# A two-block network on one core: gates inside the value and residual products, one chain for both gates, bf16 three-part biases, and a new order of steps

## The chip, the cores and the metric

The kernel runs on one core of a Trainium2 chip. Its time is the device time of one launch in microseconds (us). The median of three runs of the kernel before is 563.08 us (561.6 to 563.08). PE is TensorE, DVE is VectorE, ACT is ScalarE, POOL is GpSimd and SP is SyncE. Each engine runs its own instructions in the order in which they are written, and engines wait for each other on semaphores.

## The reference

Input x is 16 sequences of 256 tokens of 128 features, 4096 tokens in all. Two blocks follow each other; each is `x = x + s * silu(ffn)` with s and ffn computed from the layer norm of x.

```python
# block 0
xn = layernorm(x)
q, k, v = xn @ W_qkv.T                       # per sequence, linear attention
q, k = relu(q) + eps, relu(k) + eps
s = (q @ (k.T @ v)) / (q @ sum(k) + eps) @ W_out.T + b_out
gates = softmax(xn @ gate_w)                 # 8 experts, 2 largest
tok_w = sum of the 2 largest; sel = which experts
ffn = tok_w * sum over the selected e of (gelu(xn @ w1[e] + b1[e]) @ w2[e] + b2[e])   # 64 hidden each
x = x + s * silu(ffn)
# block 1
xn = layernorm(x)
K, V, Q = xn @ theta_K.T, xn @ theta_V.T, xn @ theta_Q.T
for each token of a sequence:                # TTT layer, a recurrence over 256 tokens
    g = 2/128 * (W @ k + b - v);  W -= LR * outer(g, k);  b -= LR * g;  s = W @ q + b
P = softmax(xn @ Wg), the 2 largest, normalised to sum 1
ffn = sum over the selected e of P[e] * (gelu(xn @ W1[e] + b1[e]) @ W2[e] + b2[e])    # 512 hidden each
x = x + s * silu(ffn)
```

## The kernel before

**Tiles and groups.** A tile is 128 tokens; four tiles (two sequences) are a group, and there are 8 groups. Everything is fp32 unless said otherwise, and a TensorE product in fp32 shows as two matmul instructions.

**The first pass** works through the groups in periods. Its order of steps is written out by hand in `PERIOD` (L318) and `CLOSE` (L328), and every engine walks the same lists in `first_pass` (L340) and does its part of each step in its own `work`. A step has a stage letter; in period p stage A works on group p, B on p-1, C on p-2 and D on p-3 (`LAG`, L316). A is block 0's norm (`ln0`), transposes (`xt0`), gate logits (`lg0`), attention (`k`, `v`, `q`, `kv`, `att`), the choice of experts (`sel0`, `tok0`) and its transpose (`selT`). B is block 0's experts (`hid0 0` to `hid0 3`, `y0`), the sum into x (`mix0`), block 1's norm (`ln1`), transposes (`xt1`) and gate logits (`lg1`). C is the first half of the TTT layer, solved as a triangular system per tile: key and query products (`kT`, `qT`), their Gram matrices (`gram_n`, `gram_q`, `gram_x`), the right-hand side (`resid`), and the inverse built up in levels of doubling block size (`half1`/`join1` to `half3`/`join3`), and beside it gate 1 (`sel1`, `pw1`), each token's rank in its experts (`rank`), and the sending of token rows to the experts' regions in DRAM (`copies`, `send 0` to `send 3`: indirect DMAs from POOL's queue). D is levels 4 to 6 (`half4` to `join6`, with the transposes `turn`), the two solves (`u1`, `cross`, `u2`) and the output `out`. PE does the products, ACT copies most results out of PSUM, DVE does norms, gates, masks and the joins, POOL adds biases and masks on SBUF and sends.

**Both gates** run the same chain of small DVE operations of 32 elements per partition, one after the other in a period: `shifted` (L1146), `two_largest` (L1156), `softmax` (L1173). Their logits are products of their own with 8 columns (L678, L745).

**Biases of block 0's experts.** `hid0` adds 0 or minus HUGE to hidden units of experts not chosen by a bf16 product with `selT_b` (L726); `y0` adds the output bias by an fp32 product of `selT` and `b2_l0` (L734).

**The unit stage.** When all rows are sent, expert by expert, units of 256 rows are loaded from DRAM into a ring of four by SP (L419 to L426), transposed on PE (`turn`, L854), multiplied (`hid`, L861: 4 products of 256 columns), put through gelu on ACT (`gelus`, L1036), multiplied again (`out`, L874: 8 products of 128 columns), biased and weighted on DVE (`results_of`, L1357) and scattered to DRAM by POOL (`send_results`, L583). h1T, the gelu results of one unit, is a single buffer: gelu j of the next unit waits until `out` has counted `h1_free` for k = j. On PE the order is hid(u+1), turn(u+2), out(u), hid(u+2), and hid waits for gelus of the unit before it, since their PSUM banks are reused. The first eight units stand in `CLOSE`, interleaved with the last D steps; the rest are loops. 36 units run in all.

**The end** reads the results back, adds the two choices of each token, takes silu, multiplies by the TTT output and adds to x.

## Time and profile before

| What | us |
|---|---|
| median of 3 runs | 563.08 |
| profiled execution, whole | 563.21 |
| its span, first to last instruction | 561.5 |
| one full period of the first pass (217.80 to 256.07) | 38.27 |
| the loops of the unit stage (424.18 to 529.60) | 105.42 |
| mean granted clock of TensorE, share of full speed | 0.932 |

The span is the time between the first and the last instruction of the core. The profile gives for each engine its busy time, and for TensorE the clock it was granted, as a share of 2.4 GHz (1.00 is 2.4 GHz, 0.50 is 1.2 GHz). Matmuls are pipelined: the distance between the starts of two steps is what the first of them costs; the busy time of a step also holds its tail.

### The profile page before, as it was taken

What the parts mean: (1) busy time and instruction counts of PE and PEld (TensorE: products, weight loads), DVE (VectorE), ACT (ScalarE), POOL (GpSimd) and SP (SyncE); (2) the same over time, 40 slices, a digit from 0 to 9 for tenths busy, and PEclk for the clock granted to TensorE, in tenths of its full rate; (3) what the DMA queues carried; (4) which work ended last, traced back from release to release, by engine and by line L of the source; (5) the groups of instructions that cost most, each with busy time, mean ns of one, the idle gap of its engine ahead of it and who ended that gap; (6) DMA issues with size and microseconds to landing.
All of it is one profiled execution on the core that took longest, in us unless ns stands there. A gap on an engine that the chain in (4) does not pass through costs nothing. (4 is left out here: it accounts for less than half of the span.)

```text
span 561.5 us, 10856 instructions
## 1 busy us (share of the span) xinstructions
PE 486.9 (87%) x3342; PEld 421.1 (75%) x3342; DVE 340.4 (61%) x1326; ACT 219.0 (39%) x494; POOL 211.7 (38%) x288
## 2 busy tenths in 40 slices
PE   5559588899999999999999996878999999999724
PEld 2437477689798797897897985777989899898711
DVE  6344679789888898898886766221233334434427
ACT  2233333334434424434345221113365565554502
POOL 9200131441633624516327246300454545544510
PEclk9989889899999999999999987577999999999957
DMA  7995000000000000000000001320222222222267
GB/s 201 327 165 64 0 2 11 19 11 11 21 11 11 21 21 10 20 11 20 11 11 19 20 16 39 79 51 1 56 54 69 67 71 75 68 68 62 63 223 244
DMA packets 36575, 32.58 MB, mean 58 GB/s; under 512 B 5248, under 2 KB 29358, under 8 KB 36527
## 3 DMA queue, kind: packets, MB, share of 16 engines
q1 hardware_dynamic: 31808, 22.96, 17.2%
q0 software_dynamic: 4352, 8.99, 4.9%
q8 instruction: 25, 0.41, 0.3%
q14 instruction: 24, 0.19, 0.1%
q10 hardware_dynamic: 366, 0.04, 0.1%
HBM read 16.63 MB, written 15.34 MB: 57 GB/s over the span
## 5 line engine op out<-in xcount | busy, mean ns | idle before, releaser
L588 POOL DMA_INDIRECT results<-nat,y_to x72 | 70.4, 978 | 87.4 <-DVE nat L1377 73.0
L571 POOL DMA_INDIRECT routed<-send,slot x64 | 63.0, 984 | 69.8 <-DVE slot L1298 46.1
L868 PE MATMUL psA<-xuT,w_all 128*128 128x256 f32 x288 | 71.3, 393 | 2.8 <-ACT h1T L1043 2.4
L1043 ACT ACTIVATE h1T<-psA,b1T 128x256 f32<-128x256 f32 x144 | 63.8, 474 | 5.0 <-PE psC L880 2.1
L1349 DVE TENSOR_SCALAR xu<-ring 128x256 f32 (+1 forms) x38 | 11.3, 296 | 84.0 <-DMA ring<-routed 60.6
L868 PEld LDWEIGHTS psA<-xuT,w_all 128*128 128x128 f32 x288 | 52.7, 198 | 11.0 <-issue 2.0
L880 PE MATMUL psB<-w_all,h1T 128*128 128x128 f32 x288 | 56.5, 278 | 1.8 <-DVE nat L1362 1.5
L880 PE MATMUL psC<-w_all,h1T 128*128 128x128 f32 x288 | 55.7, 275 | 0.0
L880 PEld LDWEIGHTS psB<-w_all,h1T 128*128 128x128 f32 x288 | 43.6, 192 | 3.2 <-issue 3.1
L880 PEld LDWEIGHTS psC<-w_all,h1T 128*128 128x128 f32 x288 | 43.7, 192 | 0.0
L1034 ACT ACTIVATE xuT<-psB 128x256 f32<-128x256 f32 x37 | 14.2, 383 | 61.9 <-PE psB L858 31.0
L580 POOL TENSOR_TENSOR s<-s,bias_rows 128x512 f32<-128x512 f32 x8 | 10.1, 1261 | 67.9 <-ACT s L1029 67.9
L733 PE MATMUL psB<-w_l,hg0T 128*128 128x128 f32 x256 | 34.3, 277 | 0.8 <-ACT hg0T L978 0.8
L725 PE MATMUL psB<-xnT,w_l 128*128 128x512 f32 x64 | 34.7, 626 | 0.0
L576 POOL TENSOR_TENSOR s<-s,bias_rows 128x512 f32<-128x512 f32 x8 | 10.1, 1265 | 62.8 <-ACT s L972 62.8
L733 PEld LDWEIGHTS psB<-w_l,hg0T 128*128 128x128 f32 x256 | 31.2, 192 | 1.5 <-ACT hg0T L978 1.5
L813 PE MATMUL psC<-xinvT,pn 128*128 128x64 f32 x192 | 28.1, 295 | 3.2 <-issue 2.0
L799 PEld LDWEIGHTS psD<-xinv,nT 128*128 128x128 f32 x192 | 25.6, 203 | 6.0 <-issue 3.7
L813 PEld LDWEIGHTS psC<-xinvT,pn 128*128 128x128 f32 x192 | 26.7, 215 | 3.9 <-issue 3.8
L799 PE MATMUL psC<-xinv,nT 128*128 128x64 f32 x192 | 28.0, 293 | 1.7 <-DVE xinv L1321 1.5
L799 PE MATMUL psD<-xinv,nT 128*128 128x64 f32 x192 | 26.7, 285 | 2.0 <-DVE xinv L1321 1.2
L799 PEld LDWEIGHTS psC<-xinv,nT 128*128 128x128 f32 x192 | 25.9, 209 | 3.3 <-DVE xinv L1321 2.2
(248 smaller groups left out, 1075.8 us busy)
## 6 DMA issues: line engine op xcount, KB each, us to landing
ring<-routed SPq DMA_DIRECT2D x38, 130.0 KB
w_all<-results SPq DMA_DIRECT2D x16, 256.0 KB, 5.1
routed<-ring SPq DMA_DIRECT2D x24, 130.0 KB, 9.1
w_all<-in_L_ffn_W_dram SPq DMA_DIRECT2D x1, 2048.0 KB, 14.9
out_dram<-x_all SPq DMA_DIRECT2D x8, 256.0 KB, 2.3
results<-nat,y_to POOLq DMA_INDIRECT x72
routed<-fill SPq DMA_DIRECT2D x8, 130.0 KB, 3.8
routed<-send,slot POOLq DMA_INDIRECT x64
```

The costliest lines, as they stand in the source:

```text
L571: pool.indirect_dma_start(routed[:, :], bass.IndirectOffsetOnAxis(ap=slot[par][:, c, t:t + 1], axis=0), send[par][c][:, t, :], None).then_ ...
L576: pool.tensor_tensor(s0[par][:, :, :], s0[par][:, :, :], four(bias_rows[:, 0, :]), ALU.add).then_inc(S["s0_ready"], 1)
L588: pool.indirect_dma_start(results[:, :], bass.IndirectOffsetOnAxis(ap=y_to[:, par, a:a + 1], axis=0), yw[:, par, a, :], None).then_inc(S[f ...
L725: mm(psB[j % 2][:, :], w, xT0[:, :], start=True, stop=False)
L733: mm(o, hg0T[:, j, t * P:(t + 1) * P], w2_l0[:, j, :], start=(j == 0), stop=False)
L799: last = mm(packed(bank, lv)[:, t], nT[par][:, t, :], blocks(xinv[par], lv, 0)[:, t], start=True, stop=True)
L813: last = mm(packed((psC, psD)[c][1], lv)[:, t], pn[c][:, t, :], blocks(xinvT[par], lv, 1)[:, t], start=True, stop=True)
L868: last = mm(psH[j // 2][:, (j % 2) * UNIT:(j % 2 + 1) * UNIT], w1_all[:, e, j * P:(j + 1) * P], xuT[:, :], start=True, stop=True)
L880: last = mm(psY[a][:, 0:D], h1T[:, k, a * P:(a + 1) * P], w2_all[:, f * JF + k, :], start=(k == 0), stop=(k == JF - 1))
L1034: f(xuT[:, :], psX[:, 0:UNIT], ACT.Copy).then_inc(S["xuT_ready"], 1)
L1043: f(h1T[:, j, :], psH[j // 2][:, (j % 2) * UNIT:(j % 2 + 1) * UNIT], ACT.Gelu, bias=b1T[:, n:n + 1]).then_inc(S["gelu_ready"], 1)
L1349: v.tensor_scalar(xu[:, :, :], ring[:, bass.ds(u % RING, 1), :, 0:D].rearrange("p r a d -> p (r a) d"), 1.0, None, ALU.mult).then_inc(S["x ...
```

## The change

- **Gates in other products.** gate_w stands behind the value product's weights and Wg behind the residual product's: `v` and `resid` have 136 columns instead of 128, and `lg0`, `lg1` have no products of their own. `resid` moves from stage C to a stage X, right behind `xt1`. Their results lie in pairs of tiles over two banks.
- **Both gates as one.** A stage G does gate 0 of group p and gate 1 of group p-2 in one chain of operations of 64 elements per partition (`floor`, `sel`, `tok`). Stage R does ranks, slots, copies and sends.
- **Biases of block 0 in bf16.** The output bias is split into three bf16 parts that add up to it. One bf16 transpose of the choices, each three times beside a constant one, serves both `hid0` (four bf16 products of 128 columns for one of 512) and `y0` (one bf16 product per tile for one in fp32). DVE makes the parts in the opening, from twelve small loads.
- **TTT one period later**: C has lag 3 and D lag 4. `xt1` has lag 2: it stands in the period after its norm. The close has C for groups 6 and 7 and D for groups 5, 6 and 7.
- **Norm of block 0.** Moments and inverse roots of all tiles behind the first group are made in period 0; `ln0` is four scaled copies.
- **Masks, subtraction and bias sums** of `gram_q`, `resid`, `att` and `out` go from ACT and POOL to one DVE operation each, straight out of PSUM where they were there; `gram_x` is two ACT operations. `selT` is one ACT copy.
- **Level 6** works on 64x64 blocks (`half6`, `join6`), and `join6` is an ACT copy.
- **rank** is 5 bf16 products in place of 18.
- **Unit stage.** `out` does half a = 0 over all k, then a = 1, both in one bank, and DVE adds the bias in one operation.
- **Start and hand-over.** Biases come by broadcast loads instead of products; PE starts on the identity alone; SP writes the filling rows before it waits for the sent rows.
- **New order of steps** in `PERIOD` and `CLOSE`, and an own list for period 0.

```diff
+LAG = {"S": 0, "A": 0, "G": 0, "B": 1, "R": 2, "C": 3, "D": 4, "X": 2}
+OPEN0 = (
+    "A xt0", "A v", "A ln0", "S products", "S b2", "A lg0", "G floor", "G sel", "S stats1", "S stats2", "A k",
+    "S stats3", "S stats4", "A q", "A selT", "A kv", "S stats5", "G tok", "A att", "S stats6", "S stats7",
+    "S roots", "A bias0",)
+PERIOD = (
+    "D half4", "C kT", "X xt1", "C qT", "C one", "A ln0", "R landed", "D join4", "C gram_n", "A xt0",
+    "X resid", "D half5", "X lg1", "C gram_q", "A lg0", "A v", "C gram_x", "D join5", "R copies", "B hid0 0",
+    "G floor", "C half1", "G sel", "D turn", "B hid0 1", "A q", "D half6", "C join1", "B hid0 2", "D join6",
+    "B hid0 3", "D u1", "C half2", "R rank", "A k", "R slots", "D cross", "A selT", "C join2", "B y0",
+    "C half3", "D u2", "G tok", "R send 0", "A kv", "B mix0", "R send 1", "C join3", "A att", "B ln1",
+    "R send 2", "R send 3", "A bias0", "D out",)
+CLOSE = (
+    "5 half4", "6 qT", "6 kT", "7 xt1", "7 landed", "5 join4", "6 gram_q", "6 gram_n", "5 half5", "7 resid",
...
+    "7 gram_q", "7 gram_x", "6 join5", "7 half1", "6 turn", "7 join1", "6 half6", "6 join6", "7 half2", "6 u1",
+    "U first", "7 join2", "7 send 1", "7 one", "U hid 0", "6 cross", "7 send 2", "7 half3", "6 u2", "U gelu 0",
+    "7 send 3", "7 join3", "6 out", "U sent", "7 half4", "U hid 1", "7 join4", "U out 0", "7 half5", "U hid 2",
...
@@ SP @@
+            sp.wait_ge(fill_in, 16 * E)
             wait_on(sp, "rows_landed", groups)
-            for e in range(E):
-                sp.dma_start(routed[bass.ds(free[e], UNIT), :].rearrange("(a p) d -> p a d", p=P),
-                             fill[:, e % 2, :, :]).then_inc(fill_in, 16)
-            sp.wait_ge(fill_in, 16 * E)
@@ PE work @@
                     for t in range(TILES):
-                        last = mm(psA[1][:, t * E:(t + 1) * E], xT0[:, t * P:(t + 1) * P], gate0[:, :],
-                                  start=True, stop=True)
...
+                        last = mm(pairs(psA)[:, t // 2, t % 2, 0:D + E], xT0[:, col(t)], wv_gate0[:, :],
                                   start=True, stop=True)
                     last.then_inc(S["v0_ps"], 1)
...
-                    mm(psB[j % 2][:, :], expert_of[:, j, :], selT_b[par][:, :], start=False,
-                       stop=True).then_inc(S["hid0_ps"], 1)
+                    for t in range(TILES):
+                        last = mm(psB[:, j % 2, col(t)], expert_of[:, t, j, :], selT[par][:, :], start=False,
+                                  stop=(t == TILES - 1))
+                    last.then_inc(S["hid0_ps"], 1)
...
-                        last = mm(o, selT[par][:, t * P:(t + 1) * P], b2_l0[:, :], start=False, stop=True)
+                        last = mm(o, selT[par][:, :], b2_x[:, t, :], start=False, stop=True)
...
+                elif step == f"half{LEVELS - 1}":
+                    for t in range(TILES):
+                        last = mm(psD[HALF:P, 0, t * HALF:(t + 1) * HALF], nT[par][0:HALF, t, HALF:P],
+                                  xinv[par][0:HALF, t, 0:HALF], start=True, stop=True)
...
@@ PE out(u, f, e) of the unit stage @@
                 wait_on(pe, "yb_ready", u)
-                for k in range(JF):
-                    wait_on(pe, "gelu_ready", u * JF + k + 1)
-                    for a in range(HALVES):
-                        last = mm(psY[a][:, 0:D], h1T[:, k, a * P:(a + 1) * P],
+                for a in range(HALVES):
+                    for k in range(JF):
+                        if a == 0:
+                            wait_on(pe, "gelu_ready", u * JF + k + 1)
+                        last = mm(psB[:, 1, col(a)], h1T[:, k, a * P:(a + 1) * P],
                                   w2_all[:, f * JF + k, :], start=(k == 0), stop=(k == JF - 1))
-                    last.then_inc(S["h1_free"], 1)
+                        if a:
+                            last.then_inc(S["h1_free"], 1)
@@ DVE work @@
+                elif step == "ln0":
+                    if g == 0:
+                        moments(stats0, mv0, 0, TILES, 0)
+                        inverse_roots(rstd0, mv0, 0, TILES)
+                    else:
+                        wait_on(dve, "xt0_ps", g)
+                    normalise(xn, g * TILES, mv0, rstd0, g * TILES, "xn0_ready")
...
+                elif step == "sel":
+                    ready("d_ready")
+                    ts = gate_tiles(g)
...
+                elif step == "tok":
...
+                    v.tensor_tensor(gates_of(tok_w[par]), m, z, ALU.mult).then_inc(S["tok_ready"], 1)
+                    if g >= GATES_LAG:
+                        c = slice(TILES, GT)
+                        ready("tok_ready")
+                        link(v.tensor_scalar(norm[:, :], tok_w[par][:, c], NORM_EPS, None, ALU.add))
...
+                        v.tensor_tensor(send[(g - GATES_LAG) % 2][:, :, :, COL_W], top[:, :, c],
+                                        twice(norm[:, :]), ALU.mult).then_inc(S["weights_ready"], 1)
...
+                elif step == "resid":
+                    ready("res_ps")
+                    v.tensor_tensor(by_pair(res[g % XBUFS][:, :, :]), pairs(psB)[:, :, :, 0:D],
+                                    by_pair(four(cb0[:, :])), ALU.subtract).then_inc(S["res_ready"], 1)
```

## Rows read from the trace of the kernel before

**Rows 1.** The page: busy us (share of the span) and instructions.

```profile
PE 486.9 (87%) x3342; PEld 421.1 (75%) x3342; DVE 340.4 (61%) x1326; ACT 219.0 (39%) x494; POOL 211.7 (38%) x288
```

**Rows 2.** Stages: length, busy time per engine (instructions), clock, DMA share, GB/s.

```profile
217.80:256.07 38.27, 37.39 (x298) 32.77 (x298) 33.14 (x129) 16.07 (x37) 15.60 (x17) 1.00 0.05 15
...
330.98:379.16 48.18, 36.62 (x210) 33.91 (x210) 20.05 (x72) 8.31 (x19) 20.03 (x22) 0.71 0.23 53
...
379.16:424.18 45.02, 41.89 (x279) 38.30 (x279) 11.32 (x53) 19.91 (x49) 14.21 (x15) 0.93 0.15 40
...
424.18:529.60 105.42, 102.79 (x704) 92.66 (x702) 41.95 (x192) 60.09 (x138) 52.83 (x55) 1.00 0.25 68
```

**Rows 3.** PE in order, one full period: start, busy, step, wait before.

```profile
226.85 0.95 PE L678 MATMUL psA<-gate,xnT 128*128 128x8 f32 x8
...
227.66 1.08 PE L799 MATMUL psD<-xinv,nT 128*128 128x64 f32 x8
...
233.56 0.46 PE L821 MATMUL psD<-ident,xinvT 64*128 64x64 f32 x4
...
233.95 1.11 PE L799 MATMUL psC<-xinv,nT 128*128 128x64 f32 x8
...
237.62 0.39 PE L734 MATMUL psB<-b_l,selT 128*128 128x128 f32 x2
...
237.85 1.06 PE L733 MATMUL psB<-w_l,hg0T 128*128 128x128 f32 x8
...
241.20 0.20 PE L755 MATMUL psB<-sel_b,before 128*128 128x8 bf16 x2
...
241.56 1.14 PE L683 MATMUL psA<-wkT,xnT 128*128 128x128 f32 x8
...
250.09 0.60 PE L706 MATMUL psA<-ident,sel 128*8 128x128 f32 x4
```

**Rows 4.** DVE in order, the same period.

```profile
244.71 0.69 DVE L1248 TENSOR_TENSOR mix<-s,gg 128x512 f32<-128x512 f32 x1
...
248.77 0.85 DVE L1121 BATCH_NORM_STATS2 stats<-x_all 128x6 f32<-128x128 f32 x4
...
252.58 1.11 DVE L1142 TENSOR_SCALAR send<-x_all,mv,rstd 128x128 f32<-128x128 f32 x4
```

**Rows 5.** ACT in order, the same period.

```profile
241.40 1.14 ACT L984 ACTIVATE gg<-psB,tok_w 128x128 f32<-128x128 f32 x4 [5.03 <-PE psB L734]
```

**Rows 6.** PE in order: the waits before xt0 in two periods.

```profile
71.33 0.95 PE L673 MATMUL psA<-ident,xn 128*128 128x128 f32 x4 [2.09 <-DVE xn L1142]
...
224.39 0.65 PE L673 MATMUL psA<-ident,xn 128*128 128x128 f32 x4 [0.88 <-DVE xn L1142]
```

**Rows 7.** Stretches around waits of PE, columns as in rows 2.

```profile
318.00:322.00 4.00, 3.26 (x22) 3.10 (x22) 3.36 (x9) 0.50 (x2) 2.09 (x2) 0.84 0.10 33
...
406.00:412.00 6.00, 4.92 (x37) 4.51 (x36) 1.44 (x7) 2.81 (x8) 2.24 (x3) 1.00 0.13 33
...
68.00:76.00 8.00, 5.91 (x31) 4.70 (x29) 4.94 (x18) 2.23 (x4) 1.26 (x2) 0.79 0.01 3
```

**Rows 8.** PE in order: the first transposes of the pass.

```profile
18.58 1.09 PE L673 MATMUL psA<-ident,xn 128*128 128x128 f32 x4 [3.51 <-POOL mask_lv L520]
```

**Rows 9.** PE in order: the first and the last hid of the loops.

```profile
420.45 1.89 PE L868 MATMUL psA<-xuT,w_all 128*128 128x256 f32 x8
...
524.57 1.89 PE L868 MATMUL psA<-xuT,w_all 128*128 128x256 f32 x8
```

**Rows 10.** PE in order: out of one unit and the next hid.

```profile
460.30 0.39 PE L880 MATMUL psB<-w_all,h1T 128*128 128x128 f32 x2
...
460.52 0.39 PE L880 MATMUL psC<-w_all,h1T 128*128 128x128 f32 x2
...
462.08 1.89 PE L868 MATMUL psA<-xuT,w_all 128*128 128x256 f32 x8
```

**Rows 11.** ACT in order: the four gelus beside them.

```profile
460.95 1.81 ACT L1043 ACTIVATE h1T<-psA,b1T 128x256 f32<-128x256 f32 x4
```

More of the change, by code:

```diff
@@ L356, in first_pass @@
                 else:
-                    g = groups - 2 if stage == "D" else groups - 1
-                    work(step, g, g % 2)
+                    work(step, int(g))
         MAX_UNITS = (CHOICES * tokens) // UNIT + MIN_UNITS * E
@@ new lines, in work @@
+                    ready("selb_ready")
+                    if g + GATES_LAG < groups:
+                        wait_on(pe, "q0_ready", g + GATES_LAG + 1)
+                    else:
+                        wait_on(pe, "s0_raw", groups)
+                        if g + GATES_LAG > groups:
+                            wait_on(pe, "rank_read", g)
+                    mm(rank_ps, before[:, :], sel_b[:, :], start=True, stop=False)
+                    for s in range(TILES):
+                        rest = TILES - s
+                        last = mm(rank_ps[:, (s + 1) * E:].rearrange("p (t e) -> p t e", e=E), ones_b[:, :],
+                                  sel_b[:, s * E:(s + 1) * E].unsqueeze(1).broadcast_to([P, rest, E]),
+                                  start=False, stop=(s == TILES - 1))
@@ new lines, in moments, with inverse_roots @@
+            def moments(stats, mv, first, n, x_first):
+                for t in range(n):
+                    last = v.bn_stats(stats[:, first + t, :], x_all[:, x_first + t:x_first + t + 1, :])
+                link(last)
+                for t in range(n):
+                    last = v.bn_aggr(mv[:, first + t, :], stats[:, first + t, :])
+                link(last)
+            def inverse_roots(rstd, mv, first, n):
+                ts = slice(first, first + n)
+                r, a, ve, sd = rstd[:, ts], nt_a[:, 0:n], var_e[:, 0:n], seed[:, 0:n]
+                link(v.tensor_scalar(ve, mv[:, ts, 1], LN_EPS, None, ALU.add))
+                link(v.tensor_scalar(sd, ve.bitcast(I32), 1, None, ALU.logical_shift_right))
+                link(v.tensor_scalar(r.bitcast(I32), sd, -1.0, float(RSQRT_SEED), ALU.mult, ALU.add))
@@ L1187, in ready, with work @@
+            def work(step, g):
+                par = g % 2
+                group = slice(g * TILES, (g + 1) * TILES)
                 def ready(name, per=1, k=1):
                     wait_on(dve, name, g * per + k)
-                def link_in(stage):
-                    def link(ins):
-                        ins.then_inc(order[stage], 1)
-                        links[stage] += 1
-                        dve.wait_ge(order[stage], g * CHAIN[stage] + links[stage])
-                    return link
@@ L1298, in work @@
+                    ready("rank_read")
+                    link(v.tensor_tensor(pick[:, :, c], choice[:, :, c], twice(place[:, :, :]), ALU.mult))
+                    link(v.tensor_reduce(slot_f[:, :, :], pick[:, :, c], AX.X, ALU.add))
                     v.tensor_copy(slot[par][:, :, :], slot_f[:, :, :]).then_inc(S["slots_ready"], 1)
-                    assert links["C"] == CHAIN_C, links
-                    if isinstance(g, int) and g == groups - 1:
+                    if g == groups - 1:
@@ L1360, in results_of @@
                 wait_on(dve, "yw_ready", u)
[L1361 to L1363 removed]
+                v.tensor_tensor(yb[:, :, :], tiles(psB[:, 1, :], HALVES),
+                                b2_all[:, f:f + 1, :].broadcast_to([P, HALVES, D]),
+                                ALU.add).then_inc(S["yb_ready"], 1)
                 wait_on(dve, "y_landed", u - 1)
```

882 lines of the change are left out of this document (437 added, 445 removed), and 21 rows, old and new, of tables (CLOSE, PERIOD).

## The prediction

> **What bounds the kernel now.** I read the page first: TensorE (PE) is busy 87% of the span, VectorE (DVE) 61% [rows 1]. That is an average over stages, so I cut the span into stages next [rows 2]. A full period of the first pass (all four stages A to D in it) lasts 38.27 us, with PE busy 37.39 and DVE 33.14: PE bounds it, and DVE has little to spare. There are five such periods in a row, equal within 0.02 us. The close (330.98 to about 420) is different: from 330.98 to 379.16 the granted clock is 0.71, so PE is neither full nor fast. The unit stage has PE busy 102.79 of 105.42 at clock 1.00: pure PE. Then I read one period in order of time, where the distance from one start to the next is what a step costs PE (the busy column holds the pipeline's tail and overstates it).
>
> The profiled execution took 563.21 us for a span of 561.5, so 1.7 lies around it; the median of the runs shown, 563.08, is the same number for this purpose. I sum against 563.2.
>
> **PE work in a period.** Four logit products of 8 columns cost 227.66 - 226.85 = 0.81, as much as four of 128 columns would: eight passes of 0.1. Both gates' sets go (2 x 0.81), and the value and residual products grow from 128 to 136 columns, 6% on about 0.9 each, +0.1: together -1.5. y0's bias product costs 237.85 - 237.62 = 0.23 per tile in fp32; in bf16 it is one pass instead of two and one column a cycle: priced by hid0's bf16 products (512 columns at 0.22) it is 0.06. Four tiles: -0.7. The four selection transposes (L706, 0.60 long) become one [rows 3]: -0.3. rank goes from 18 instructions in 0.36 to 5: -0.25. hid0's bf16 product of 512 columns becomes four of 128 with four weight loads; rank's 18 products with a load each take 20 ns apiece, so loads don't bound it: 0, at worst +0.1 per step, +0.4 a period. half6 and join6 work on 64x64 blocks: each between 0 and 0.45 less than their 0.85; I take 0.2 each, -0.4. Sum: -3.2 of some 37.1, so 33.9 of PE work in a full period (bounds 33.4 to 34.6).
>
> The Trainium skill ("TensorEngine Tiling (Array Packing)", Key Properties) says that a change of tiling mode drains TensorE, which speaks against the 64x64 form of half6 and join6. The one 64x64 step here, the turn, takes 233.95 - 233.56 = 0.39 for four passes, 0.1 each although only 64 columns wide, which fits a small drain [rows 3]. By that rule alone the two steps gain nothing, and a period would be 0.4 longer, 1.6 over four.
>
> **DVE work in a period.** Removed: the first norm's moments and roots (the second norm's, 252.58 - 248.77 = 3.8, are the same instructions [rows 4]), one of two gate chains (about 3.6 of 9.5: the links stay, with 64 elements instead of 32), join6's copy 0.45. Added: masks, subtraction and two bias sums that POOL or ACT did, four operations of 512 elements at 0.69 (as L1248 [rows 4]): +2.7. DVE falls from 33 to about 29 busy; ACT loses some 3. POOL loses five operations of 1.27. None of these is on the path by its total; the order is.
>
> **Where the period waits then.** The new order puts xt1 third in the next period, and it waits for the second norm, the last long work of DVE. I walk from the start Y of y0. PE: y0 3.8, half3 0.9, u2 0.5, kv 0.9, join3 0.9, att 0.95, out 2.4, half4 0.85, kT 0.95: xt1 could start at Y+12.1. ACT: y0 lands at Y+4.0, scaled copy 1.14 [rows 5] to 5.2, then half3, u2 and kv stand before the tanh of mix0, which ends at 7.3. DVE: k, slots (1.05), cross, join2 end at Y+2.3, the merged softmax and weights (14 links, 3.2) at 5.5, mix0 three operations of 0.69 with the second waiting for the tanh: 8.75; join3 1.1, att 0.4, norm 4.9 (moments from 248.77 to the last of the four outputs, 253.69 [rows 4]): Y+15.15. So xt1 waits 3.0. If DVE never waited it would be 13.4 and the wait 1.25. I take 2.2.
>
> Idle time has a second price. After 2.09 us without work the granted clock went to half rate for about 3.5 us (a mean of 0.79 in the 8 us around it), but not after the 0.88 of every full period, nor after 1.08 (4.92 busy of 6.00) [rows 6, 7]. 2.2 lies at the first of these: half the periods, at 1.7 each. Period: 33.9 + 2.2 + 0.9 = 37.0; bounds 35.2 (1.25 and no slow clock) and 38.7 (3.05 and always). Four such periods instead of five 38.27: per period -1.27, over the four -5.1.
>
> **The thin periods.** TTT one period later leaves periods 2 and 3 thinner. Before, the second norm of group 0 is done at 61.65 and that of group 2 at 138.9 (one period before 177.2, two before 215.4, three before 253.69): 77.3. With no C and D in period 2 my walk (xt1, ln0, xt0, resid, v at half rate, hid0, q, k, y0, tail) gives 25.3; period 3 has C but not D, 33.5. Together 58.8, so -18.5. Period 8 has no A: 33.1 against 34.5, -1.4. The thinned work comes back in the close.
>
> **Opening.** PE's first transposes waited 3.51 for POOL's masks until 18.58 [rows 8]; now they wait for the identity alone and start near 13.4, 5.2 earlier. But DVE then has the split of the bias (17 operations, 4.0), and moments and roots of 28 tiles (seven of about 1.4, whose statistics are 0.85 [rows 4], and 2.5 of roots: 12.3, 7.5 more than one group's 4.8). These fall partly into DVE's waits. hid0 of group 0 no longer fills the gap before period 1. By walk, group 0's second norm is done at 63.8 instead of 61.65: +2 (bounds -3, all hidden, and +6, nothing hidden). The twelve bias loads end before DVE asks for them, unless the large weight loads hold them up.
>
> **Close.** Before: from the norm of group 7 (326.5) to the first hid of the loops (420.45 [rows 9]) 94.0, with 59.3 of full-rate PE work; 34.7 are lost, over half of it at half rate. After: C and D of groups 6 and 7, D of 5: 75.6 of work. Two chains alternate, PE has something to do in most gaps: my walk has PE at the first turn after 34, with 3.4 of gaps, and the rows are sent in time (slots at +16.4, eight sends of 1.27, then 3 to 6 to land; the fillings no longer follow them). I add 4 for half rate, 7 for unit waits and chain ends: lost 14.4, close 90. -4 (bounds -11, lost 7, and +16, lost 34.7).
>
> **Unit stage.** out used to do both halves for each k; now half a=0 runs over all k, then a=1, and only a=1 frees h1T. Before: out starts at 460.30, its fourth pass for k=0 ends at 460.52 + 0.39 = 460.91, gelu starts at 460.95, 0.65 after out's start [rows 10, 11]. Now k=0 is free after passes 9 and 10: 4 x 0.223 + 0.39 = 1.28, gelu at 1.32 to 1.39, two gelus 0.42 + 0.47, done at 2.28, and PE answers 0.14 later: the next hid starts 2.42 after out's start, not 462.08 - 460.30 = 1.78. So +0.63 per unit, at every unit, because PE had no idle time and gelu sits in the loop. 27 steps from 420.45 to 524.57 [rows 9]: +17 (bounds: +12 if some of the 3.3 of odd waits there are hidden in it, +17).
>
> **Sum.** +2 - 18.5 - 5.1 - 1.4 - 4 + 17 = -10.0: 553.2.
>
> **Rivals.** (1) Slower: the clock. The wait before xt1 takes its full 3.05 and the half rate lasts 6.8 us each time, as it did from 320.6 to 327.4 in period 8 (the fall is in [rows 7]): 33.9 + 3.05 + 3.4 = 40.35 per period, +13.4 over four and +3.4 in periods 3 and 8: 570. It turns the sign from a period of 39.5 on. For it: the fall in period 8 came after two waits of about 0.5 only. Against: full periods hold 1.00 through 0.88. (2) The unit wait does not come, since gelu is not held as I think: -17, 536. For it: nothing but my reading of one semaphore; against, gelu's start 0.04 after the fourth pass [rows 10, 11]. (3) No wait before xt1, PE bounds the period at 34.0: -3.0 times four and -2.8 twice, 535.6. For it: my durations on DVE are strung together; against, even DVE without waits is late. (4) The close loses its 34.7 as before (DVE in order behind a late unit load, half rate again): +20, 573.5. For it: it has more steps of 64 columns, which ran at 0.71.
>
> Chances: forecast 0.42 (its own range 543 to 563), (1) 0.17, (2) 0.12, (3) 0.14, (4) 0.15. About 0.3% is what a measurement of this kernel tells from no change, here 561.4 to 564.8. Faster: 0.35 of the forecast's and the 0.26 of (2) and (3), 0.61; the same 0.09, the forecast's upper end and the mild ends of (1); slower 0.30. The range that leaves 2 in 10 out: 535 to 573.
>
> **What would show it.** Opening: L673's successor near 13.4. A full period 35 to 39 long with PE waiting at xt1 on DVE's norm, and a granted clock under 1.00 there. The logit products gone, y0 near 3.8. Unit stage: starts of hid 4.37 apart instead of 3.73, PE idle before each on ACT's h1T. Close: granted clock above 0.8. I am wrong if hid stays at 3.73, or if xt1 starts right behind kT.

## The result and the profile after

The kernel before takes 559.5 us (median of 20 runs, 553.3 to 564.7), the changed kernel 562.7 us (20 runs, 560.0 to 567.3). The ratio is 1.008, 95% interval 1.0056 to 1.0103: the change makes the kernel 0.8% slower. The forecast was 553.2, so the sign was wrong, though the time lies inside the range. Its -10.0 was counted from 563.2, the level of the first three runs; from 559.5 it would have been 549.5.

The profiled execution of the changed kernel took 561.8 us for a span of 560.0. That of the kernel before, with 563.2, is above most of its own 20 runs; so I compare a second pair of profiles too, taken on one chip (runs before_same_chip and after_same_chip below). First the page of the changed kernel, part 1, then the granted clock in 40 slices of the span (9 stands for 90% of full speed or more):

```profile
PE 466.1 (83%) x3176; PEld 396.9 (71%) x3176; DVE 306.9 (55%) x1097; ACT 188.7 (34%) x464; POOL 168.5 (30%) x251
...
PEclk9767697978989999979989958799999999999968
```

Against [rows 1] TensorE (PE) has 20.8 us less to do, VectorE (DVE) 33.5, and nothing came of it: the busy share fell, the time did not. The stages say where it went. This is the view of stretches of the changed kernel, columns as in [rows 2]; the cuts are at the starts of xt1 for groups 0 to 7 (65.81 to 314.61), then inside the close, at the first hid of the loops (409.11) and at the last (524.07).

```profile
0.00:65.81 65.81, 30.39 (x153) 23.13 (x153) 43.47 (x197) 15.14 (x35) 20.66 (x83) 0.79 0.74 172
65.81:91.66 25.85, 19.00 (x118) 14.77 (x119) 17.75 (x73) 8.52 (x20) 6.79 (x9) 0.83 0.04 13
91.66:124.65 32.99, 29.92 (x201) 24.32 (x201) 23.61 (x83) 11.44 (x27) 10.91 (x14) 0.86 0.06 20
124.65:164.36 39.71, 36.66 (x276) 31.32 (x277) 26.23 (x87) 13.29 (x33) 9.85 (x14) 0.93 0.05 14
164.36:203.03 38.67, 35.63 (x276) 30.29 (x276) 26.31 (x88) 13.30 (x33) 9.91 (x13) 0.96 0.05 15
203.03:240.33 37.30, 34.25 (x277) 29.43 (x277) 26.25 (x88) 13.30 (x33) 9.98 (x13) 0.98 0.05 16
240.33:280.22 39.89, 36.84 (x276) 31.50 (x277) 26.47 (x88) 13.30 (x33) 9.91 (x13) 0.93 0.05 14
280.22:314.61 34.39, 32.15 (x239) 26.58 (x239) 21.94 (x77) 10.96 (x26) 10.04 (x12) 0.96 0.05 17
314.61:359.52 44.91, 42.23 (x283) 39.69 (x284) 24.39 (x77) 10.06 (x26) 10.73 (x14) 0.76 0.17 47
359.52:409.11 49.59, 45.52 (x322) 41.04 (x322) 15.00 (x50) 18.03 (x48) 11.60 (x12) 0.98 0.13 36
409.11:524.07 114.96, 107.97 (x703) 95.92 (x703) 38.87 (x163) 52.65 (x136) 51.99 (x54) 1.00 0.22 63
```

Two things are to be seen. The four full periods (124.65 to 280.22) execute the same instructions, 276 or 277 on PE, and last 37.30, 38.67, 39.71 and 39.89: they follow the clock column, 0.98, 0.96, 0.93, 0.93. Before, they were equal at 1.00. And the unit stage has PE waiting, 107.97 busy of 114.96 at clock 1.00, where it was all but full [rows 2].

The stages of both pairs, in us (before, then after):

| stretch | forecast | first pair | same-chip pair |
|---|---|---|---|
| opening, to xt1 of group 0 | +2 | 61.6, 65.8: +4.2 | 64.0, 67.9: +3.9 |
| the two thin periods | -18.5 | 77.3, 58.8: -18.4 | 79.4, 59.5: -19.9 |
| four full periods | -5.1 | 153.1, 155.6: +2.5 | 153.2, 155.8: +2.6 |
| xt1 of group 6 to the loops' first hid | -5.4 | 128.4, 128.9: +0.5 | 124.5, 128.9: +4.4 |
| 27 unit steps | +17 | 104.1, 115.0: +10.8 | 102.0, 115.0: +13.0 |
| tail | 0 | 36.9, 36.0: -0.9 | 36.5, 35.8: -0.7 |
| sum | -10 | -1.4 | +3.3 |

The last row is the difference of the spans; the rows above it are rounded one by one. The second pair agrees with the medians (+3.2). The thin periods gave what they were to give. The units took back the most, 10.8 to 13.0, then the opening with 4 and the full periods with 2.5. How much the close took depends on the profile of the kernel before: its own close was 3.9 us shorter in the second one.

Who ends the waits of PE shows in the view of waits of the changed kernel, first 124.65 to 314.61, then the unit stage (us in total, times, longest):

```profile
PE psB L712 <- DVE send L1141: 13.5, 5, 3.0
PE psC L802 <- ACT pn L1007: 0.3, 1, 0.3
```

```profile
PE psA L857 <- ACT h1T L1032: 7.3, 28, 0.3
```

The first is the wait before xt1 for the second norm, 3.05 for each of groups 3 to 6 (the fifth, 1.3, is that of group 2 at the edge). Before, no full period had it. The rows of these four waits (start, busy, step, wait before) show one more thing:

```profile
164.36 1.12 PE L712 MATMUL psB<-ident,send 128*128 128x128 f32 x4 [3.05 <-DVE send L1141]
203.03 0.66 PE L712 MATMUL psB<-ident,send 128*128 128x128 f32 x4 [3.04 <-DVE send L1141]
240.33 1.12 PE L712 MATMUL psB<-ident,send 128*128 128x128 f32 x4 [3.04 <-DVE send L1141]
280.22 1.12 PE L712 MATMUL psB<-ident,send 128*128 128x128 f32 x4 [3.05 <-DVE send L1141]
```

The same four transposes are busy 1.12 us behind three of the waits and 0.66 behind the one that ends at 203.03: there the clock stayed full, and no half rate is seen until 238.9, inside the next wait. That is the period of 37.30. So one trace already holds the same wait with and without half rate behind it. (The first full period, behind the wait of 1.3, is at half rate until 129.7; there the clock had fallen at 119.6, behind a wait of 1.76 before half4.)

The second row of the waits is the one before hid for the first gelus, once a unit. Outside these two, the view of waits shows 0.3 us in these stretches of PE.

### The profile page after: what moved, and what is told of

It reads as the page before. It is cut to its first block, busy times and chain, and to the rows that moved or that the text cites. A ratio compares the mean times of both kernels' runs of the same rounds, so it can differ in the third digit from the quotient of the medians.

```text
span 560.0 us, 10211 instructions
## 1 busy us (share of the span) xinstructions
PE 466.1 (83%) x3176; PEld 396.9 (71%) x3176; DVE 306.9 (55%) x1097; ACT 188.7 (34%) x464; POOL 168.5 (30%) x251
## 4 chain that ended last, share of the span: by engine, by line
PE 66%; DVE 16%; issue 5%; ACT 5%; DMA 3%; ACTq 2%; POOL 1%; SPq 0%; DVEq 0%; POOLq 0%
PE psA L857 13%; PE psB L870 7%; PE psB L694 6%; PE psB L706 5%; PE psC L788 4%; PE psC L802 4%; ACT h1T L1032 3%; PE psD L802 2%; DVE stats L1122 2%; PE psC L747 2%; PE psA L647 1%; PE psC L751 1%; PE psB L847 1%; DVE send L1141 1%; PE psD L788 1%
## 5 line engine op out<-in xcount | busy, mean ns | idle before, releaser
L551 POOL DMA_INDIRECT routed<-send,slot x64 | 65.9, 1030 | 191.9 <-DVE send L1250 141.5
L870 PE MATMUL psB<-w_all,h1T 128*128 128x128 f32 x576 | 70.5, 275 | 0.6 <-ACT h1T L1032 0.6
L870 PEld LDWEIGHTS psB<-w_all,h1T 128*128 128x128 f32 x576 | 67.1, 192 | 0.9 <-ACT h1T L1032 0.8
L857 PEld LDWEIGHTS psA<-xuT,w_all 128*128 128x128 f32 x288 | 52.6, 193 | 20.8 <-ACT h1T L1032 12.6
L1032 ACT ACTIVATE h1T<-psA,b1T 128x256 f32<-128x256 f32 x144 | 56.4, 474 | 26.4 <-PE psB L870 26.4
L962 ACT ACTIVATE hg0T<-psB,b1T 128x512 f32<-128x512 f32 x32 | 22.0, 687 | 33.3 <-PE psB L696 33.3
L712 PE MATMUL psB<-ident,send 128*128 128x128 f32 x32 | 8.0, 398 | 26.7 <-DVE send L1141 26.7
L712 PEld LDWEIGHTS psB<-ident,send 128*128 128x128 f32 x32 | 5.1, 198 | 33.4 <-DVE send L1141 33.4
L1386 DVE TENSOR_TENSOR nat<-psB,b_all 128x256 f32<-128x256 f32 x36 | 15.3, 424 | 23.6 <-PE psB L870 23.6
L696 PEld LDWEIGHTS psB<-selT,expert_of 128*128 128x128 bf16 x128 | 10.0, 99 | 18.9 <-issue 18.9
L1341 DVE STREAM_TRANSPOSE xinv<-xinvT 128x512 f32<-128x512 f32 x32 | 22.8, 712 | 1.1
```

The source lines that it names most:

```text
L551: pool.indirect_dma_start(routed[:, :], bass.IndirectOffsetOnAxis(ap=slot[par][:, c, t:t + 1], axis=0), send[par][:, c, t, :], None).then_ ...
L857: last = mm(psA[:, j // 2, (j % 2) * UNIT:(j % 2 + 1) * UNIT], w1_all[:, e, j * P:(j + 1) * P], xuT[:, :], start=True, stop=True)
L870: last = mm(psB[:, 1, col(a)], h1T[:, k, a * P:(a + 1) * P], w2_all[:, f * JF + k, :], start=(k == 0), stop=(k == JF - 1))
L962: f(hg0T[:, j, :], psB[:, j % 2, :], ACT.Gelu, bias=b1T[:, HT + j:HT + j + 1]).then_inc(S["hg0_ready"], 1)
L1032: f(h1T[:, j, :], psA[:, j // 2, (j % 2) * UNIT:(j % 2 + 1) * UNIT], ACT.Gelu, bias=b1T[:, n:n + 1]).then_inc(S["gelu_ready"], 1)
L1341: v.transpose(xinv[par][:, :, :], xinvT[par][:, :, :]).then_inc(S[f"xinv{lv}_ready"], 1)
```

## The experiments

Each edit is shown against the kernel named; the step lists are shared by all engines.

**The unit stage.** out_k_outer undoes one part of the change, before_a_outer does that part alone.

```
 # out_k_outer, in out() of the changed kernel
-for a in range(HALVES):
-    for k in range(JF):
-        if a == 0: wait_on(pe, "gelu_ready", u * JF + k + 1)
-        last = mm(psB[:, 1, col(a)], h1T[:, k, ...], ...)
-        if a: last.then_inc(S["h1_free"], 1)
+for k in range(JF):
+    wait_on(pe, "gelu_ready", u * JF + k + 1)
+    for a in range(HALVES):
+        last = mm((psB[:, 1, 0:P], psC[:, 0, 0:P])[a], h1T[:, k, ...], ...)
+    last.then_inc(S["h1_free"], 1)
```

> The changed kernel with one part undone: in the unit stage the second product (out) runs k outermost again, both halves of the unit for each k, each half in a PSUM bank of its own, and h1T is given back after every k (and so two bias additions of 128 columns on VectorE where there was one of 256). Theory A, the unit order is a cost of its own: TensorE waits 0.4 to 0.5 us before each hid on ACT's first gelus only because h1T comes free after the whole first half. Then the step of a unit goes from 4.26 to 3.73 us, 27 steps and the seven outs in the close with it: 10.8 less in the stage, up to 3 more in the close, so 548 to 552. Rival B: the units are longer because of something else that the change did (the extra work of the close behind them, unit loads that come late, the one bias addition): then the step stays above 4.1 and the time is 560 to 563.

> The kernel before with this part alone done: out runs half a=0 over all k and then half a=1, and h1T is given back only from the second half; the two PSUM banks and the two bias additions stay. Theory A: the step of a unit goes from 3.73 to about 4.26 us and the kernel is 11 to 17 us slower than before (27 steps of 0.41 to 0.63), 570 to 576. Rival B (the order costs nothing by itself, TensorE's own work in the step bounds it): 559 to 562.

Measured: out_k_outer 555.1 us, ratio to the kernel before 0.9785 (0.974 to 0.983); before_a_outer 578.8, ratio 1.022 (1.0175 to 1.0263). The kernel before took 568.3 us beside these two, on another chip. The changed kernel was not measured there, so neither the times nor the ratios can be set against its own exactly; the stage itself can. By the loops' stretch (out_k_outer first, then before_a_outer, columns as in [rows 2]):

```profile
414.10:517.89 103.79, 102.72 (x704) 92.41 (x703) 40.56 (x188) 58.87 (x136) 51.47 (x54) 1.00 0.25 69
```

```profile
424.00:539.82 115.82, 108.48 (x706) 96.01 (x705) 39.95 (x191) 53.61 (x138) 53.27 (x55) 1.00 0.23 62
```

The one edit takes 27 steps from 115.0 to 103.8, the other puts the old kernel from 104.1 to 115.1 (the stretch shown begins 0.7 ahead of the first hid). Both directions are seen, and the step is 4.26 with and 3.8 without, whatever stands around it. The rival is out. (late_xt1_k_outer below does the same edit beside its partner on one chip: 550.9 to 536.2.) How the 4.26 comes about, by PE in order in the changed kernel (start, busy, step, wait), and ACT beside it:

```profile
460.20 1.99 PE L857 MATMUL psA<-xuT,w_all 128*128 128x256 f32 x8 [0.26 <-ACT h1T L1032]
462.03 0.38 PE L847 MATMUL psB<-ident,xu 128*128 128x128 f32 x2
462.25 1.95 PE L870 MATMUL psB<-w_all,h1T 128*128 128x128 f32 x16
464.46 0.48 PE L857 MATMUL psA<-xuT,w_all 128*128 128x256 f32 x1 [0.26 <-ACT h1T L1032]
```

```profile
463.57 1.20 ACT L1032 ACTIVATE h1T<-psA,b1T 128x256 f32<-128x256 f32 x3 [0.73 <-PE psB L870]
```

out starts at 462.25, the first gelu 1.32 later, the next hid 2.21 later; before, 0.65 and 1.78 [rows 10, 11]. PE, ACT and the one buffer h1T form a ring with little slack: the first gelu starts 0.67 later behind out, and the next hid 0.43 later.

**The wait before xt1 and the clock behind it.** tanh_first exchanges "A kv" and "B mix0" in PERIOD. fill_pe sets useless products before the wait:

```
 elif step == "xt1":
+    for _ in range((6, 5, 1, 3, 3, 3, 3, 0)[g]):
+        mm(psB[:, 1, :], wqT, xT0[:, :], start=True, stop=True)
     ready("xn1_ready")
```

> The changed kernel with two neighbours in the period's order exchanged: mix0 now stands before kv, so ACT does the tanh of the gate before the copy of kv. Theory A: the tanh is late behind kv, the middle of mix0 on VectorE waits for it, the second norm ends with it and TensorE waits for the norm before xt1. Then the wait of 3.05 us before xt1 falls by about one copy, 0.6 to 0.8, and the period by that or more: 0.8 times five periods, 4, so 557 to 559.5; more, to 553, if the half rate behind the wait goes too. Rival B: VectorE's own work bounds the chain (k, slots, cross, tok, join3, att before and in it) and the tanh is not late by that much: wait 2.8 to 3.05, time 561 to 563. Rival C: kv is itself on the path (att waits for it): PE then waits for kv's copy before att and the time is the same or 1 to 3 more.

> The changed kernel with useless fp32 products of 512 columns (about 0.86 us each) set in TensorE's queue just before its wait for xt1: 6, 5, 1, 3, 3, 3, 3, 0 for groups 0 to 7. They fill most of the wait and write a part of PSUM that xt1 overwrites; the output does not change. Theory A: the fall of the granted clock to half rate behind the wait is a price of its own, and it comes from TensorE's standing still. Then the full periods show a granted clock of 0.98 to 1.00 and each is 1 to 2 us shorter (38.9 to about 37.3), 5 to 8 us over the periods, so 554 to 558. Rival B: the half rate costs nothing because TensorE catches up against other waits (its later waits shrink when it is slow): clock 1.00 and the time the same, 561 to 564. Rival C: the clock falls whatever TensorE does there (it is set by something else, such as the small products of 64 columns that come before): clock 0.93 to 0.96 as now and the same time.

> The kernel of the run fill_pe once more. There the granted clock was 1.00 in every full period and the periods were 38.8 us all the same, because in that execution ACT's copy of half4 started some 6 us late in each of the four and join4 on TensorE then waited 1.5 for it; the trace shows no cause, and the kernel before was 9 us slower than usual in that call. Theory A, half rate has a price of its own: without that late copy the periods are 37.3 (38.8 less 1.5), where the changed kernel has 38.9 in the mean with 0 to 5.8 us of half rate in each; 1.6 times four is 6.4 less, and 1 to 3 more in the thin periods, so 554 to 557, a ratio of about 0.993 to the kernel before where the changed one has 1.006 to 1.008. Rival B, half rate costs nothing and the late copy belongs to the filled kernel: periods of 38.8 again, ratio 1.00 to 1.01.

tanh_first: 563.5 us, ratio 0.993 (0.990 to 0.996); fill_pe: 562.6, ratio 0.991 (0.988 to 0.994), both on the chip with 568.3. In tanh_first the wait is 2.04 to 2.17 instead of 3.05, about as expected, and the full periods still show clocks of 0.92 to 0.96 and last 38.1 to 40.7 (the 40.7 has a late copy of ACT in it, see below): a shorter wait, and half rate behind it all the same. What tanh_first gains as a whole stays open, since the changed kernel was not measured beside it. fill_pe was confounded. Its clock is 0.96 in the first full period and 1.00 in the other three, but its periods last 38.8; ACT's copy of half4 started late in all four. The view of waits names a releaser that it does not know:

```profile
ACT pn L1010 <- remote: 24.4, 4, 6.1
```

out_k_outer, whose periods are those of the changed kernel, has the same row with the same numbers, tanh_first one such wait of 6.9, the changed kernel none. So the filling is not needed for it, and I ran the kernel again, on another chip. fill_pe_again: 553.3 us, ratio 0.9885 (0.985 to 0.992), without such a row. Its full periods:

```profile
124.16:161.45 37.29, 36.82 (x282) 30.59 (x282) 26.08 (x87) 13.31 (x33) 9.86 (x14) 1.00 0.05 15
161.45:198.75 37.30, 36.82 (x282) 30.57 (x283) 26.26 (x88) 13.30 (x33) 9.91 (x13) 1.00 0.05 15
198.75:236.04 37.29, 36.82 (x283) 30.56 (x283) 26.23 (x88) 13.31 (x33) 9.98 (x13) 1.00 0.05 16
236.04:273.33 37.29, 36.82 (x283) 30.57 (x283) 26.24 (x88) 13.31 (x33) 9.91 (x13) 1.00 0.05 16
```

With 24 products more the kernel is some 9 us faster than the changed one, 6.4 of it in the full periods. Nothing but what PE does while it waits was altered, and the periods fall from 38.9 in the mean to 37.3, which is what the changed kernel's own third period takes, the one without half rate. So half rate is a price of its own, 1.6 a period in the mean (2.4, 1.4, 0 and 2.6 in the four), and it goes when PE does not stand still; rivals B and C are out.

The half rate in the four periods of the changed kernel is 2 x (1 - clock) x length, 5.6 + 3.1 + 1.5 + 5.6 = 15.8 us, and the loss against the filled kernel is 155.6 - 149.2 = 6.4. The Trainium skill ("TensorE: Matmul & The Clock Gate", Terms) puts the penalty at the time at reduced rate times the share of pulses left out, here half, which would be 7.9. The runs show 6.4, a little less: in slices of 1 us, some 2.3 of the half rate lie inside the waits before xt1, where they cost nothing, and half of the remaining 13.4 is 6.7.

after_same_chip and before_same_chip are the two kernels themselves, beside the next two.

> The changed kernel itself, unaltered, so that the other runs of this chip have their partner: on this kind of comparison the kernel before has taken 559.5 and, on another chip, 568.3. Theory A: the change costs about the same everywhere, 0.8% over the kernel before in the same call. Rival B: the two kernels move differently from chip to chip (the changed one has more chains of short steps, the one before is bound by TensorE), and the ratio here lies outside 1.000 to 1.015. In the profile: unit step 4.26 us, 3.05 before xt1, half rate behind it in two to four of the four full periods.

> The kernel before itself, for its profile on the same chip as the other runs: full periods of 38.27 us at granted clock 1.00, first products of the units 3.73 apart, and a ratio of 1.00 to the kernel before. If the total is near 568 as in the last call, the profile shows where the 9 us over 559 lie: theory A, in the close and the opening, where the clock falls; rival B, everywhere.

The changed kernel: 563.0, ratio 1.006 (1.003 to 1.0085); the one before 561.0, ratio 1.001 (0.998 to 1.005). The result repeats, and their stages are in the table above.

**Taking the wait away.** late_xt1, against the changed kernel:

```
-"D half4", "C kT", "X xt1", "C qT", ...   "A kv", "B mix0", ...   "A bias0", "D out"
+"D half4", "C kT", "C qT", "X xt1", ...   "B mix0", "A kv", ...   "D out", "A bias0"
```

> The changed kernel with three neighbours exchanged in the period's order: mix0 before kv (as in the run tanh_first), the product qT before xt1 on TensorE, and TTT's out before bias0 on VectorE. Theory A: the wait before xt1 is what is left when TensorE has nothing before it; a tanh earlier takes 0.85 of it (as tanh_first measured, 3.05 to 2.17) and qT before it 0.95 more, so it is 1.2; a wait of that size leaves the granted clock at 1.00 as 1.08 did in the kernel before. The full periods go from 38.9 to 35.5, 35.0 to 36.5, or 10 to 15 us over the periods in all: 548 to 553 where the changed kernel takes 563. Rival B: join4, which waits for VectorE's last addition of out, takes over the wait (0.7 and more): periods of 36.5 to 37.5. Rival C: the half rate comes all the same, for the small products: periods of 38 and more.

> late_xt1 and out_k_outer in one: the three exchanges of the period and, in the unit stage, out with k outermost in two banks. If both causes are what they seem, the gains add, since the one lies in the periods and the other in the units: 10 to 15 and 11 to 14 less than the changed kernel, so 0.955 of it, about 537, and 3 to 5% under the kernel before. If it is less than the larger of the two alone, one of them is not what it seems.

late_xt1: 550.9 us, ratio 0.985 (0.981 to 0.989). late_xt1_k_outer: 536.2, ratio 0.953 (0.947 to 0.959). Beside the changed kernel's 563.0 the first takes off 12, the second 15 more, where 10 to 15 and 11 to 14 were expected. Three of the full periods of late_xt1_k_outer:

```profile
162.36:198.55 36.19, 34.67 (x276) 29.51 (x276) 26.47 (x88) 13.38 (x33) 9.73 (x13) 1.00 0.05 16
198.55:234.75 36.20, 34.67 (x276) 29.52 (x276) 26.47 (x88) 13.38 (x33) 9.80 (x13) 1.00 0.05 16
234.75:270.83 36.08, 34.67 (x276) 29.52 (x276) 26.34 (x88) 13.38 (x33) 9.63 (x13) 1.00 0.06 18
```

The wait is 1.3, the clock stays full, the period is 36.2 (the first full period, behind a wait of 2.3, is 37.2 at 0.95). I expected 35.5. Of 3.05 + 34.25 only 1.1 went although 1.75 of wait did: behind the start of xt1, 0.4 more passes between gram_n and xt0 than in the changed kernel (the view shows 0.23 of it as a wait for DVE's first norm), and 0.1 each ahead of join4 and gram_n. Rival B, a wait of 0.7 and more at join4, did not come.

**The opening, and what became of its gain.** open_b2_late moves "S b2" out of OPEN0 into the first period, behind "A xt0". b2_period_fill is that kernel with fillings before xt1 (5, 3, 2, 1, 1, 1, 1, 0 for groups 0 to 7).

> late_xt1_k_outer with the split of the bias into three bf16 parts (17 operations of VectorE, 4.0 us) moved from the middle of the opening to the first period, behind the first norm of group 1, where VectorE waits. Theory A: the split is in the chain of the opening (the chain of waits goes through the bias loads and the split until 19.4), so the first norm of group 0's second layer ends 2 to 4 earlier than 67.8 and the time falls by as much, 532 to 534. Rival B: VectorE waits for TensorE and the weight loads in the opening anyway, and what makes it longer is the 28 tiles of statistics; then 0 to 1 less, 535.5 to 537. Rival C: the split is late for the first y0: 1 to 3 more.

> open_b2_late with useless fp32 products of 512 columns (0.86 us) before TensorE's wait for xt1: 5, 3, 2, 1, 1, 1, 1, 0 for groups 0 to 7. open_b2_late ended its opening 4.5 us earlier (xt1 of group 0 at 63.3 where late_xt1_k_outer had 67.8) and was no faster; its full periods were 37.3 to 39.1 with 3.4 to 6.8 us of half rate in each, where late_xt1_k_outer had 36.2 with none. Theory A: the gain was given back by the clock alone, after waits of 1.2 to 1.5 us; with the waits filled every full period is 36.2 at clock 1.00 and the thin ones are 1 to 2 shorter, so 528 to 531. Rival B: the order is slower by itself since the split came in (VectorE later in every period): periods of 37.3 at clock 1.00, 534 to 537.

open_b2_late: 536.5 us, ratio 0.958 (0.954 to 0.962), no gain over late_xt1_k_outer. Yet xt1 of group 0 starts at 63.3 instead of 67.8: the split of the bias had been on the opening's path, 4.5 us of it. (b2_period_fill and all_fill start it at 62.8. In the run both, with the same opening, it starts at 66.4: there DVE's first four scaled copies took 4.00 us instead of 1.40. So 4.5 is what three of the four traces show.) The full periods of open_b2_late show where the 4.5 went:

```profile
120.35:159.41 39.06, 37.54 (x277) 32.75 (x277) 25.49 (x87) 13.38 (x33) 10.52 (x13) 0.91 0.05 16
159.41:197.11 37.70, 36.18 (x276) 31.05 (x276) 26.69 (x88) 13.39 (x33) 9.85 (x13) 0.95 0.05 15
197.11:234.51 37.40, 36.11 (x277) 31.14 (x277) 26.67 (x88) 13.38 (x33) 9.67 (x13) 0.95 0.05 14
234.51:271.82 37.31, 36.12 (x276) 31.14 (x277) 26.44 (x88) 13.38 (x33) 9.64 (x13) 0.95 0.05 17
```

They last 5.8 us longer than those of late_xt1_k_outer. The first stands behind a wait of 2.3, as there. The other three stand behind waits of 1.52, 1.53 and 1.28 where late_xt1_k_outer has 1.3, with the same steps, and now the clock falls some 2 us behind the start of xt1 in each. b2_period_fill: 529.7 us, ratio 0.944 (0.940 to 0.948); its full periods are 35.8, 36.6, 36.3 and 36.2 at clock 1.00, the thin ones 25.6 and 30.7. Theory A holds: with the clock full, the full periods are 0.8 shorter in all than those of late_xt1_k_outer instead of 5.8 longer, so it was the clock that had eaten the gain.

**The close.** close_fill and both set products of 256 columns before waits of PE in the close; all_fill is b2_period_fill with these and two more.

```
+FILL = {("xt1", 7): 4, ("half1", 6): 1, ("turn", 5): 1, ("join6", 5): 1, ("half3", 6): 1}
+for _ in range(FILL.get((step, g), 0)):
+    mm(psA[:, 0, 0:256], wqT, xnT0[(groups - 1) % 2][:, 0:256], start=True, stop=True)
```

> late_xt1_k_outer with useless fp32 products of 256 columns (0.43 us at full rate) set before the waits of TensorE at the start of the close: four before xt1 of group 7, one each before half1 and half3 of group 6 and turn and join6 of group 5. Theory A: the half rate of 17 us from 313.9 on comes from TensorE's standing still shortly before (1.99 before xt1 at 303.1, then 0.58, 0.42 and 0.56 by 315.2); filled, the clock stays at 1.00 to 331 and the close falls from 89 to about 81 to 83, the kernel to 528 to 531. Rival B: it comes from the small products themselves (blocks of 64 columns and of half the array), of which the close has a stretch without the large ones: clock 0.5 there as before and the fillings cost 0 to 2 us, 536 to 538.

> open_b2_late and close_fill in one kernel. Where the two gains are what their runs show they add, as they lie 250 us apart; by theory A of both 524 to 528, by the rivals of both 536 to 538.

> b2_period_fill with the fillings of close_fill (four products of 256 columns before xt1 of group 7, one each before half1 and half3 of group 6, turn and join6 of group 5) and two more, before turn and join6 of group 6. Theory A: with the periods at full rate and the half rate gone from the first 20 us of the close, as close_fill showed, both gains hold: 523 to 527. The two further fillings also take away the 10 us of half rate that close_fill still had from 336.7 on: then 519 to 523. Rival B: a fall that is filled in one place comes in the next, as in close_fill where one of 10 us began at 336.7: the close keeps 10 to 17 us of half rate and the kernel comes to 526 to 530.

close_fill: 532.0 us, ratio 0.950 (0.9455 to 0.955). The start of the close without the fillings (late_xt1_k_outer):

```profile
303.10:313.90 10.80, 9.80 (x83) 9.34 (x84) 7.74 (x22) 2.53 (x7) 2.37 (x5) 0.97 0.04 14
313.90:320.00 6.10, 5.54 (x38) 5.26 (x36) 3.85 (x17) 1.52 (x4) 0.00 (x0) 0.50 0.00 0
320.00:331.00 11.00, 10.58 (x52) 10.28 (x52) 5.71 (x28) 0.77 (x2) 3.88 (x4) 0.53 0.20 60
```

and with them:

```profile
302.30:314.00 11.70, 11.44 (x96) 10.25 (x94) 8.81 (x25) 2.75 (x8) 2.82 (x6) 1.00 0.04 13
314.00:331.00 17.00, 16.26 (x127) 13.98 (x126) 12.79 (x49) 4.04 (x10) 7.41 (x8) 1.00 0.22 64
331.00:345.00 14.00, 12.61 (x80) 11.45 (x79) 4.30 (x8) 3.29 (x9) 0.97 (x1) 0.70 0.25 68
```

From 314 to 331 PE does 90 matmul instructions, nearly all at half rate, in the one and 127 at full rate in the other, with the same small blocks among them. So the small blocks alone do not bring the half rate; with PE's waits filled (2.0 before xt1 at 303.1, 0.6 and 0.4 at 310.6 and 312.1) it does not come there. But a fall of 10 us begins at 336.7, earlier than the next one of late_xt1_k_outer (7 us from 344.1), and the close (xt1 of group 7 to the loops) went from 92.7 to 88.8 only. That is the traces; the totals, 0.953 and 0.950 of the kernel before, are within each other's intervals. Either way it is less than the 5 to 8 I expected. both: 534.1, ratio 0.953 (0.949 to 0.957), not told apart from either of its parts: the 524 to 528 of theory A did not come. In its trace two full periods more than in close_fill fell to clock 0.95, as in open_b2_late, and the opening was the slow one named above. all_fill: 526.1 us (522.0 to 529.5), ratio 0.939 (0.935 to 0.943). Its full periods are all at clock 1.00; 6.8 us of half rate are left in the close from 334.9 on. It is the lowest of all, though its interval touches that of b2_period_fill: 6% under the kernel before, and 37 us under the changed one (563.0), each beside a kernel before of 560 to 561. The 519 to 523 for no half rate in the close did not come.

## Why the prediction was wrong

**The full period, the step that failed.** The forecast walked the period, got a wait of 3.0 before xt1, and then took 2.2, a value between that and the bound without DVE's waits. The trace shows 3.05. That it fits so well is in part luck: both ends of the wait lay 0.1 later than walked, PE at 12.2 behind the start of y0 and the norm at 15.3. PE's work at full rate is 37.30 - 3.05 = 34.25 where 33.9 was forecast. The rest is the clock: I counted half rate in every second period at 1.7, 0.9 a period; fill_pe_again shows 1.6 a period. Together 34.25 + 3.05 + 1.6 = 38.9 instead of 37.0: 0.35 from the work, 0.85 from the wait, 0.7 from the clock, 7.6 over four periods. Measured was +3.2 in all; without these 7.6 the kernel would have been faster than before. The mechanism was named, as rival (1), whose place was right and whose price (40.35 a period) was too high; the choice inside my own bounds was the mistake. I had a walk and no reason against it but its consequence. It was not the only term large enough for the sign: the close below was missed by 6 to 10, and the units, forecast 4 to 6 too dear, hid part of both.

**The close.** Forecast 90 from group 7's norm, measured 94.5. The two chains do fill PE, as forecast (42.23 busy of 44.91 from 314.61 on), but at a clock of 0.76. I put half rate at 4; it lay from 324.6 to 341.8 and from 355.0 to 361.8, 24 us, so some 12 lost. I had argued that little waiting means little half rate; in late_xt1_k_outer a wait of 2.0 and two of about 0.5 went before such a stretch, and close_fill, with them filled, had none there. The starting value was off too: the 94.0 came from a profile whose close was 3.9 longer than that of before_same_chip.

**The opening.** Forecast +2, measured +4.2 and +3.9. open_b2_late gives back 4.5: the split, 5.0 us here where I had 4.0, and which I had let fall partly into DVE's waits, was on the path nearly whole. PE's first transposes did start early, at 13.36 as forecast, but it was of no use: the gate chain could not begin before the split ended, at 19.97, and PE waited 4.49 for it.

**The unit stage.** Right in mechanism and place, shown from both sides. Forecast 4.37 a step, measured 4.26: the next hid comes 2.21 after out's start, not 2.42, since the first gelu starts at the early end of what I gave (0.07), the two gelus take 0.84 together instead of 0.89 (queued, they start 0.36 apart) and hid follows 0.05 behind them instead of 0.14. The first product of hid takes 0.1 more behind its wait. Against the old step, 3.73 at its best and 3.78 to 3.86 in the mean, it costs 10.8 to 13.0; my bound of +12 for hidden odd waits was the better number.

**The thin periods.** -18.5 forecast, -18.4 measured in the first pair and -19.9 in the second. There the walk was used as it came out.

**The 64x64 steps.** In the forecast I took 0.2 off for each. The changed kernel's half6, eight passes on 64x64 blocks between steps of the full array, takes 381.39 - 380.78 = 0.61 where the old form took 0.85:

```profile
380.78 0.68 PE L770 MATMUL psD<-xinv,nT 64*64 64x64 f32 x8
381.39 1.99 PE L857 MATMUL psA<-xuT,w_all 128*128 128x256 f32 x8
```

The Trainium skill ("TensorEngine Tiling (Array Packing)", Key Properties) says that a change of mode drains the engine. If it does here, the drain is small enough to leave a gain of 0.24 a step, a little more than I took.

## What to carry to other kernels

When an engine that was always busy gets its work cut, look for the first wait that opens on it and price the clock behind that wait, not the wait alone: here 1.3 us of wait could be free or cost 1.1 more, and 3.05 cost between nothing and 2.6 more. A useless product in the wait is a cheap experiment that tells the two prices apart, and sometimes the cheapest cure. And when your own walk through a trace gives a number, start from it: here it was 3.0 for 3.05 and 2.42 for 2.21. A buffer that is handed back later in a ring with little slack costs most of its delay at every turn, here 0.40 to 0.53 of 0.67.

## What the runs showed of the hardware

- In slices of 1 us the granted clock was 0.50 or 1.00, but for the slices in which it changed. It fell after single waits of 1.3 to 3 us and, in the close, after one of 2.0 and two of about 0.5, and stayed full where products of no use stood in these waits (the full periods of fill_pe_again and all_fill, 314 to 331 in close_fill). The length of the wait does not decide alone: a wait of 1.3 left the clock full in late_xt1_k_outer, waits of 1.28 to 1.53 did not in open_b2_late, with the same steps around; in the one trace of both, it stayed full behind a wait of 1.51 (161.15) and fell behind the next of 1.51 and one of 1.30; and the changed kernel kept it through one wait of 3.04 of four. What decides between them I cannot say from these runs.
- Since it falls by such small differences, an improvement in one place can be lost later, as the 4.5 us of the opening were in the full periods of open_b2_late, and small waits must be judged in the kernel as a whole.
- The same kernel before took 559.5 to 561.3 us in four sets of measurements and 568.3 in one. In that one, all four profiles show ACT starting a copy 4 to 7 us late, one to four times, with no releaser known; the first profile of the kernel before has such a wait of 3.5 too, at the same step as before_a_outer its 3.9, and the changed kernel and the ten later profiles have none. Whether this and the longer times belong together stays open.
